# Cross-attention on one Trainium2 core: half of the first context over ScalarE's DMA queue, and Z's splits dealt in between the chunks of the first context

## The reference, cut to what matters

```
g     = g_w X + g_b          (256 x 1024)
theta = theta_w x + theta_b  (256 x 1024)
phi   = phi_w X + phi_b      (256 x 1024)
W     = theta^T phi / 1024
y     = (W g^T)^T
out   = gamma * (w_w y + w_b - mean) / sqrt(var + 1e-5) + beta + x
```

## Time and profile before

| | us |
|---|---|
| median of 3 runs | 810.19 (809.51 to 810.68) |
| the profiled execution, its own time | 808.35 |
| its span | 806.5 |
| TensorE busy | 778.9 (97%) |
| mean granted clock of TensorE | 0.992 |

### The profile page before, as it was taken

The page is one execution under the profiler, slowest core; times in us unless marked ns, Lnnn a source line. Parts: engine busy times, 40 slices in busy tenths (PEclk is TensorE's granted clock), DMA queues, the critical chain, the costliest instruction groups (busy, mean ns, idle before and its releaser), DMA issues.

```text
span 806.5 us, 11687 instructions
## 1 busy us (share of the span) xinstructions
PE 778.9 (97%) x4045; PEld 664.8 (82%) x4045; DVE 529.1 (66%) x901; ACT 304.4 (38%) x508; POOL 535.9 (66%) x351
## 2 busy tenths in 40 slices
PE   4499999999999999999999999999999999999997
PEld 2388888888888888888888888888888888888885
DVE  3858485775848667484875848577584866758254
ACT  2545242533414353342434424243452435334121
POOL 0888577785757868575785857688575777857400
PEclk9799999999999999999999999999999999999999
DMA  8735517163360826427072541717345071640202
GB/s 217 205 107 104 210 28 216 69 172 140 79 233 1 210 101 156 156 62 249 1 208 104 121 191 42 229 41 182 130 95 217 19 212 81 161 152 1 105 1 104
DMA packets 53011, 103.10 MB, mean 128 GB/s; under 512 B 2410, under 2 KB 35844, under 8 KB 52996
## 3 DMA queue, kind: packets, MB, share of 16 engines
q1 hardware_dynamic: 52996, 102.91, 43.6%
HBM read 69.35 MB, written 33.55 MB: 128 GB/s over the span
## 4 chain that ended last, share of the span: by engine, by line
PE 95%; DVE 2%; DMA 2%; SPq 1%; issue 0%; DVEq 0%; ACT 0%
PE wbank L540 57%; PE gbank L540 36%; DMA ctx_sb<-in_ctx_dram 2%; PE wbank L659 1%; DVE ctxT_lo L422 1%; DVE ctxT L386 1%; DVE z_lo L432 0%; SPq L217 0%; SPq L208 0%; DVE wp_lo L439 0%; DVE x_sb L530 0%; DVE wt_lo L439 0%; DVEq L66 0%; ACT ctxT_hi L297 0%; DVE zb_row L435 0%
## 5 line engine op out<-in xcount | busy, mean ns | idle before, releaser
L264 POOL TENSOR_TENSOR ctxT_lo<-ctxT,ctxT_hi 128x512 fp32r<-128x512 f32 x120 | 162.7, 1356 | 195.8 <-ACT ctxT_hi L297 195.8
L272 POOL TENSOR_TENSOR ctx_sum<-ctx_sum,ctxT 128x512 f32<-128x512 f32 x112 | 171.8, 1534 | 0.9 <-POOL ctx_sum L267 0.2
L280 POOL TENSOR_TENSOR x_lo<-x_sb,x_hi 128x1024 fp32r<-128x1024 f32 x64 | 151.8, 2407 | 2.7 <-ACT x_hi L297 2.7
L297 ACT ACTIVATE mt<-wbank 128x512 fp32r<-128x512 f32 x64 | 38.3, 598 | 250.7 <-PE wbank L540 250.7
L454 DVE TENSOR_TENSOR stage<-gbank,mt 128x384 f32<-128x384 f32 x64 | 28.4, 485 | 145.9 <-PE gbank L540 145.9
L530 DVE SCALAR_TENSOR_TENSOR x_sb<-wbank,const,x_sb 128x512 f32<-128x512 f32 x112 | 79.1, 747 | 67.6 <-PE wbank L540 67.6
L540 PE MATMUL wbank<-ctxT_lo,ctxT_hi 128*128 128x512 f32 x512 | 118.7, 389 | 0.0
L297 ACT ACTIVATE ctxT_hi<-ctxT 128x512 fp32r<-128x512 f32 x128 | 79.3, 629 | 102.9 <-DVE ctxT L386 102.9
L540 PEld LDWEIGHTS wbank<-ctxT_lo,ctxT_hi 128*128 128x128 f32 x512 | 95.1, 188 | 18.7
L386 DVE STREAM_TRANSPOSE ctxT<-ctx_sb 128x512 f32<-128x512 f32 x128 | 81.7, 683 | 10.4 <-DMA ctx_sb<-in_ctx_dram 10.4
L540 PE MATMUL wbank<-x_hi,wt_hi 128*128 128x512 f32 x256 | 81.7, 400 | 0.0
(11 more groups left out here) (100 smaller groups left out, 1346.9 us busy)
## 6 DMA issues: line engine op xcount, KB each, us to landing
ctx_sb<-in_ctx_dram SPq DMA_DIRECT2D x64, 512.0 KB, 8.4
x_sb<-in_x_dram SPq DMA_DIRECT2D x16, 2048.0 KB, 7.8
out_dram<-x_sb SPq DMA_DIRECT2D x64, 512.0 KB, 2.6
x_sb<-in_L_xattn_w_w_dram SPq DMA_DIRECT2D x1, 512.0 KB, 3.8
x_sb<-in_L_xattn_g_w_dram SPq DMA_DIRECT2D x1, 512.0 KB, 3.6
phi_nat<-in_L_xattn_phi_w_dram SPq DMA_DIRECT2D x1, 512.0 KB, 13.0
stage<-in_L_xattn_theta_w_dram SPq DMA_DIRECT2D x1, 512.0 KB, 12.7
bp_row<-in_L_xattn_phi_b_dram SPq DMA_DIRECT2D x1, 128.0 KB, 11.7
```

The source lines that it names most:

```text
L264: nc.gpsimd.tensor_tensor(ctxT_lo[:, c, :], src, f(ctxT_hi[:, c, :]), ALU.subtract).then_inc(ctxT_lo_made, 1)
L272: nc.gpsimd.tensor_tensor(ctx_sum[:, :], ctx_sum[:, :], src, ALU.add).then_inc(ctxT_used, 1)
L280: nc.gpsimd.tensor_tensor(x_lo[:, k, :], x_sb[par][:, k, :], f(x_hi[:, k, :]), ALU.subtract).then_inc(x_lo_made, 1)
L297: nc.scalar.activation(dst, src, ACT.Copy).then_inc(sem_, 1)
```

## The change

ScalarE issues two of the four pieces of the first context (partitions 64 to 127) at the head of its list, and SP the other two. On ScalarE and VectorE the splits of Z's four groups no longer stand behind the eight chunks: one group goes behind each pair of chunks. On VectorE the order inside a round is: two transposes, Z's lo part, two lo parts of the context. Two waits on `ctxT_lo_made` are added ahead of the transposes that write into a used slot of the ring, and one ahead of the batches.

```diff
-            def load_ctx(b):
+            def load_ctx(b, parts=range(QT)):
                 src = ctx_in[b].rearrange("(k q) (a n) -> a q k n", q=32, a=QT)
-                for a in range(QT):
+                for a in parts:
                     sp.dma_start(ctx_sb[32 * a:32 * a + 32, :, :], src[a]).then_inc(in_ctx, 16)
...
-            load_ctx(0)
+            load_ctx(0, (0, 1))
...
+            src = ctx_in[0].rearrange("(k q) (a n) -> a q k n", q=32, a=QT)
+            for a in (2, 3):
+                act.dma_start(ctx_sb[32 * a:32 * a + 32, :, :], src[a]).then_inc(in_ctx, 16)
             act.wait_ge(ident_done, 2)
             hi(ident_r[:, :], ident[:, :], ident_r_made)
             act.wait_ge(vec_step, 2)
             nc.scalar.activation(tmp[:, 1, :], tmp[:, 0, :], ACT.Sqrt).then_inc(root_done, 1)
-            for c in range(CH):
-                ctx_hi(0, c)
-
-            for g in range(KC):
+            def z_hi_part(g):
                 act.wait_ge(work_done, 3 + g)
                 hi(z_hi[:, g, :], wbank[(2 + g) % NW][:, :], split_hi)
+
+            ctx_hi(0, 0)
+            ctx_hi(0, 1)
+            for g in range(KC):
+                z_hi_part(g)
+                if g < KC - 1:
+                    ctx_hi(0, 2 + 2 * g)
+                    ctx_hi(0, 3 + 2 * g)
...
-            for c in range(CH):
-                transpose_chunk(0, c, c >= RING)
-                if c > 0:
-                    first_lo(c - 1)
-            first_lo(CH - 1)
-            for g in range(KC):
+            def z_lo_part(g):
                 dve.wait_ge(split_hi, g + 1)
                 nc.vector.tensor_tensor(z_lo[:, g, :], wbank[(2 + g) % NW][:, :], f(z_hi[:, g, :]),
                                         ALU.subtract).then_inc(work_free, 1)
+
+            transpose_chunk(0, 0, False)
+            transpose_chunk(0, 1, False)
+            for g in range(KC):
+                z_lo_part(g)
+                first_lo(2 * g)
+                first_lo(2 * g + 1)
+                if 0 < g < KC - 1:
+                    dve.wait_ge(ctxT_lo_made, 2 * g)
+                if g < KC - 1:
+                    transpose_chunk(0, 2 * g + 2, 2 * g + 2 >= RING)
+                    transpose_chunk(0, 2 * g + 3, 2 * g + 3 >= RING)
...
             dve.wait_ge(in_bp, 16)
+            dve.wait_ge(ctxT_lo_made, CH)
```

## The result

The changed kernel takes 812.94 us (median of 12 runs, 812.05 to 813.48) against 810.14 (12 runs, 809.0 to 811.9) beside it. The ratio is 1.0034 with a 95% interval of 1.0026 to 1.0042: 2.8 us slower, clear of noise. The runs of before spread over 2.9 us, those of after over 1.4.

A forecast was written before the change was run, and what follows sets the result against it. TensorE, busy for 97% of the span, was taken as the bound, so batch 0's start decides: context arrival plus VectorE's sequence changes 0, clock adds 0.85, 810.19 + 0 + 0.85 = 811.0 us; range 809.0 to 813.5.

The forecast's parts named there:

- the signs of being wrong: Profile after: stalls far below 1 us, first transpose before 13.5 or after 17, or batch 0 starting at clock 1.00.
- Term 1: Set-up, first context's load: VectorE gets it at 14.3 in the good case or 15.9, at latest 18.25.
- every byte takes as long as now: Transfer engines at the head: w_w and g_w take 2.6 us, the context 10, ending at 14.7, seen at about 15.9.
- rival 2: First context's load: pieces finish together and late, context still at 18.25, time 813.8; chance 0.11.
- The second gate: VectorE's first split of Z waits for TensorE's first group, hence the vectors; that group done at about 17.0.
- d: Delay of the small vectors to TensorE behind ScalarE's pieces: taken as 1.2 us, bounds 0 and 3.
- rival 1: Set-up: weights come late, vectors delayed 3 us, Z done at 18.9; 812.5, or 813.4 with whole clock loss; chance 0.17.
- Term 2: VectorE's set-up from the first transpose: 22.0 us instead of 19.2, with four stalls of 1.2.
- The give-back at GpSimd: VectorE's lo parts wait less for GpSimd's adds, which run largely inside the stalls: 2 us returned.
- Sum of the first two: VectorE's set-up end: 36.3 or 37.9 by the context, 37.1 by Z; so 37.1 to 37.9, against 37.47.
- Term 3: TensorE's clock as batch 0 begins: cold at 0.50, losing 1.7 us, bounds 0.8 and 3; half, 0.85, added.
- Rival 3: Set-up faster: vectors undelayed, both context halves side by side, no clock loss against the median; 808.4; chance 0.15.

The follow-up runs named there:

- the split alone: Kernel before with only the context's transfers changed, ScalarE issuing two of the four pieces and the order kept: 810.17 us, ratio 1.001.
- the dealt kernel: Kernel before with only the order of splits changed as in the change, SP issuing all four context pieces: 811.94 us, ratio 1.0031.
- the mended transfers: Kernel before, ScalarE's two pieces issued after w_w lands, SP's later loads held until the context arrives, three met waits added: 806.41 us, ratio 0.9959.

## Why the prediction was half right

The time lies in the whole range given (809.0 to 813.5), but above the forecast's own (809.8 to 812.3). The arithmetic of VectorE held; but I gave 0.59 to no change and 0.30 to slower, and it is slower by 2.8 us. One of the signs of being wrong that I had named came: the first transpose is at 18.36, after 17. By its own steps:

- **Term 1, the context's arrival: wrong.** I put 14.3 to 15.9, with today's 18.25 as the upper bound; it is 18.36. What failed is the step "every byte takes as long as now". With ScalarE's pieces on the way w_w lands 6.6 us after its issue, not 3.8, and g_w after 8.4, not 3.6; from 6 to 9 us SP's queue moved 0.09 MB and both together 0.62, which is 207 GB/s. Added up over the windows from 2 to 11 us, all queues moved 2.19 MB, against 1.93 in the kernel before, although the idle window was filled; and SP's half of the context was still to come. This is what rival 2 has as its condition (no earlier context), for which it gave 813.8; its reason, that the pieces finish together and late, is not what happened: ScalarE's were done first.
- **The second gate: the mechanism right, the size wrong.** I took d = 1.2 with bounds 0 and 3; it is 10.48 - 5.85 = 4.6. This is rival 1, with d beyond its 3 and Z's first group done at 20.9 where it had 18.9 and my forecast 17.0. I had counted w_w's doubled time as 2 us (it is 2.8), but not that the eight tiny transfers wait on while SP's queue stands. That the pieces ahead of them are the cause is shown from both sides, by the run with the pieces behind w_w (5.86) and by the split alone (10.34); how each of them is held up is not.
- **Term 2, VectorE's sequence: right.** 22.0 from the first transpose was expected, and 22.1 is measured with the transfers of before. From the first z_lo to the end I had 19.5; the kernel after has 41.10 - 21.54 = 19.56. The stalls are 1.18 each. The give-back at GpSimd that I put at 2 is borne out from the other side: with the stalls taken out, 2.6 of their 4.7 us are lost to turns.
- **Sum of the first two.** By Z, 20.9 + 0.6 + 19.5 = 41.0 against the 41.10 measured; by the context, 18.36 + 22.0 = 40.4. So either gate alone would have upset the forecast of 37.1 to 37.9. With the right d the forecast by Z would have been about 3.5 us later.
- **Term 3, the clock: right for the profile, nearly nothing for the median.** Batch 0 did begin at 0.50 and lost 7.75 - 4.95 = 2.8 us against the profile of before; I had taken 1.7, from 3.35 us at half speed, and here the clock is back at 1.00 only at about 47.7, 6.2 us after batch 0 began. But other profiles of the old order lose 1.3 to 2.6 as well. I added 0.85 to the median, half of the 1.7, because I did not know whether the median already held a cold start; by the 51 of 71 executions above, it seems mostly to. The table leaves little room for it: the start of batch 0 moved by +3.65, less 1.2 at the end, makes +2.45 for a measured +2.8; for the dealt kernel +2.6 - 1.2 = 1.4 for 1.8; with the mended transfers -2.1 - 1.2 = -3.3 for -3.6. All ten differences follow from these two columns within 0.5 us.
- **Not foreseen: the end.** 1.2 us were saved by three more waits in VectorE's list (perhaps by the place of a fetch), and kept a start that is 3.65 us later to 2.8 us of time. Nothing in the order of the instructions hinted at it.
- **A slip.** Rival 3's sum, 810.19 less 2.0, is 808.2 and not 808.4; nothing hangs on it.

So the range held partly by luck: the late start of batch 0 by itself is worth 3.65 us, which gives 810.19 + 3.65 = 813.8, outside the range, and the end's -1.2 brought it back in. The same luck puts the time between rival 1's 812.5 and 813.4, though VectorE ended 2 us later than rival 1 had it. What stays open is how much of the rest, up to 0.5 us per kernel, is the clock; single profiles scatter by more than that.

## What to carry to other kernels

Work out what a new transfer does to those that are already on their way, above all to tiny ones with a chain behind them: a load that is wanted late and issued first cost the vectors 4.6 us. Dealing work between two engines needs a distance: place a consumer one round behind its producer, and look for what takes turns with the moved work before counting the freed time as gained. And compare medians before trusting one profile's start; the warm one here belonged to the minority.

## What the runs showed of the hardware

- Two loads to partitions 0 to 63 and 64 to 127, issued from two engines at once, moved at 347 and 348 GB/s together in two kernels, against about 210 for one alone. Issued by SP alone, the four pieces, two to each half, moved at 202 to 231 in the kernel before (9 to 17 us). The Trainium skill, SBUF — State Buffer, section "Door 1: The DMA port swizzle", says that the two halves use different ports, which agrees. The same page, section "Can I just issue two DMAs to hit both halves?", says that they serialize, with 6% gained; here they do not.
- Loads to all 128 partitions on SP's queue were held up by loads to 32 partitions on ScalarE's: 0.09 MB against 0.53 from 6 to 9 us in the kernel after, 186 to 222 GB/s in all. It was not so all the time: from 4 to 5 both queues moved alike, 0.17 and 0.18 MB, at 354 GB/s together. Why the one stretch differs from the other no run shows.
- The end of the program moved by 1.1 us through three instructions that do nothing, some 770 us ahead of it.
- With TensorE kept busy, its clock was at 0.50 as batch 0 began at 38.60, though it had been at 1.00 until 37.5 and the engine busy until 3.3 us before batch 0.
